# Preparing the first attention: query stacks in two buffers, rows normed one batch earlier, turned rows copied between the middle parts

## The reference, cut to what matters

```python
h = concatenate([token_mix(x), txt], axis=1)            # (8, 1056, 64), float32
h = h + attn(layernorm(h))                              # the first attention
def attn(x):
    qkv = (x @ qkv_w + qkv_b).reshape(B, N, 3, 8, 8)
    q, k, v = qkv[:, :, 0], qkv[:, :, 1], qkv[:, :, 2]
    attn = einsum('bnhd,bmhd->bhnm', q * 8 ** -0.5, k)
    bias = transpose(rpb_table[rel_idx], (2, 0, 1))      # by the distance of two rows
    attn = softmax(attn + bias[None], axis=-1)
    return einsum('bhnm,bmhd->bnhd', attn, v).reshape(B, N, 64) @ proj_w + proj_b
```

## Time and profile before

| what | value |
|---|---|
| median of 3 runs | 2847.63 us (2846.12 to 2851.1) |
| the profiled execution's own time | 2844.59 us |
| its span | 2842.8 us |
| mean granted TensorE clock | 0.899 of full speed |
| busy over the span | PE 88%, DVE 70%, ACT 53%, POOL 14% |
| store of qs, eight times, 1152 KB | 4.4 us to landing (median) |
| store of qT, eight times, 1056 KB | 4.4 us |
| store of kT, eight times, 1056 KB | 7.4 us |

### The profile page before, as it was taken

The page is one execution under the profiler, slowest core; times in us unless marked ns, Lnnn a source line. Parts: engine busy times, 40 slices in busy tenths (PEclk is TensorE's granted clock), DMA queues, the critical chain, the costliest instruction groups (busy, mean ns, idle before and its releaser), DMA issues. The chain is left out here.

```text
span 2842.8 us, 52541 instructions
## 1 busy us (share of the span) xinstructions
PE 2499.5 (88%) x18456; PEld 1092.8 (38%) x18456; DVE 1983.2 (70%) x5070; ACT 1519.3 (53%) x2629; POOL 400.8 (14%) x500
## 2 busy tenths in 40 slices
PE   5988657999999999997499999896679999599999
PEld 3323552333333333333333333564544444423333
DVE  5777667888888888883377776657676765266665
ACT  2331663777777777775144444334656667143443
POOL 1011210000000000002312111222100100411110
PEclk9998666999999999998599999665689999599999
DMA  2101751111111111122500100134441222701100
GB/s 75 23 15 24 239 203 58 48 48 32 48 46 34 48 41 39 48 45 48 111 12 19 25 15 21 48 94 125 154 139 61 81 62 57 155 12 30 30 21 15
DMA packets 272791, 174.02 MB, mean 61 GB/s; under 512 B 225857, under 2 KB 230786, under 8 KB 271282
## 3 DMA queue, kind: packets, MB, share of 16 engines
q1 hardware_dynamic: 262170, 151.59, 19.9%
q0 software_dynamic: 10368, 19.06, 2.2%
HBM read 96.11 MB, written 74.53 MB: 60 GB/s over the span
## 5 line engine op out<-in xcount | busy, mean ns | idle before, releaser
L1674 DVE TENSOR_REDUCE att_mpart<-ps 128x1 f32<-128x512 f32 x1024 | 635.6, 683 | 82.2 <-PE ps L1494 52.0
L1642 ACT ACTIVATE att_p<-ps 128x704 f32<-128x704 f32 x768 | 543.7, 760 | 136.1 <-PE ps L1558 131.8
L1587 PE MATMUL ps<-att_p,att_v 128*9 128x352 f32 x3072 | 300.5, 462 | 0.1
L1494 PE MATMUL ps<-att_kT,att_qT 64*128 64x512 bf16 x1024 | 276.4, 387 | 20.7 <-DMA att_qz<-qt_d 8.3
L1558 PE MATMUL ps<-att_qm,att_kT 64*128 64x352 bf16 x1536 | 251.9, 317 | 10.4 <-ACT att_p L1642 8.0
L1288 DVE TENSOR_REDUCE cau_mpart<-ps 128x1 f32<-128x512 f32 (+5 forms) x384 | 193.4, 552 | 80.3 <-PE ps L1114 60.9
L2419 ACT ACTIVATE mo_act<-ps,mo_b 128x768 f32<-128x768 f32 x176 | 156.3, 901 | 132.4 <-PE ps L2301 126.9
L2572 DVE TENSOR_TENSOR mo_g<-mo_act,ps 128x768 f32<-128x768 f32 x176 | 167.4, 951 | 77.8 <-PE ps L2336 41.2
L1255 ACT ACTIVATE cau_p<-ps 128x704 f32<-128x704 f32 (+6 forms) x272 | 171.5, 660 | 81.7 <-PE ps L1173 49.7
L2971 ACT ACTIVATE mo_act<-ps 128x1024 f32<-128x1024 f32 (+1 forms) x108 | 102.9, 953 | 195.0 <-PE ps L2885 194.8
L1558 PEld LDWEIGHTS ps<-att_qm,att_kT 64*128 64x128 bf16 x1536 | 82.8, 93 | 287.5 <-issue 278.0
(11 more groups left out here) (444 smaller groups left out, 4257.0 us busy)
## 6 DMA issues: line engine op xcount, KB each, us to landing
qs_d<-pre_qs SPq DMA_DIRECT2D x8, 1152.0 KB, 4.4
att_qs<-qs_d SPq DMA_DIRECT2D x32, 288.0 KB, 4.1
qt_d<-pre_qT SPq DMA_DIRECT2D x8, 1056.0 KB, 4.4
kt_d<-pre_kT SPq DMA_DIRECT2D x8, 1056.0 KB, 7.4
att_kT<-kt_d SPq DMA_DIRECT2D x32, 264.0 KB, 2.7
att_qT<-qt_d SPq DMA_DIRECT2D x32, 264.0 KB, 3.1
cqt_d<-cpr_qT SPq DMA_DIRECT2D x8, 1056.0 KB, 4.4
cau_qT<-cqt_d SPq DMA_DIRECT2D x16, 528.0 KB, 4.0
```

The costliest lines, as they stand in the source:

```text
L1494: mm = pe.matmul(ps[:, bank, :], qT[half(s), u, j * P:(j + 1) * P], kT[half(s), u, c * BANK:(c + 1) * BANK], start=True, stop=not near)
L1587: mm = pe.matmul(ps[32 * cg:32 * cg + DV, 7, 0:TH], v[:, u, i, s, :], p[:, r, s, :], start=i < 2, stop=i == FULL - 1)
L1642: e = act.activation(p[:, n % PRING, :, :], ps[:, bank:bank + 2, 0:TH], ACT.Exp)
L1674: red = dve.tensor_reduce(mpart[:, j, s, c:c + 1], ps[:, bank, :], AX.X, ALU.max)
```

## The change

The stacked queries get a second buffer. Rows are loaded three batches ahead, measured two batches ahead at the start of a step, and normed two batches ahead behind the fourth copy of turned queries. GpSimd takes the root of b + 2 after its middle parts, and sets up the second buffer behind root(1). ScalarE puts each of its three copies of turned rows in front of the middle parts 1, 2 and 3 of the keys, and waits for the `qs` store of two batches before in place of the last one. The loops are plain loops over b with the same steps.

```diff
@@ names @@
-        qs = nm.sb("qs", [P, NT, H * R], BF16)
+        qs2 = nm.sb("qs", [P, 2, NT, H * R], BF16)
+        qs = [qs2[:, i, :, :] for i in range(2)]
@@ SyncE @@
+            sp.wait_ge(xn_made, NT)
+            load(sp, 2, 0)
-            def step(b, par, more):
+            def step(b, par):
                 if b == 3:
                     ahead(sp, const)
-                if more:
-                    sp.wait_ge(xn_made, (b + 1) * NT)
-                    load(sp, b + 2, par)
+                if b + 3 < B:
+                    sp.wait_ge(xn_made, (b + 2) * NT)
+                    load(sp, b + 3, 1 - par)
@@ GpSimd @@
-            pool.memset(qs[:, :, :], 0.0).then_inc(zeroed, 1)
+            pool.memset(qs[0], 0.0).then_inc(zeroed, 1)
...
             pool.wait_ge(ones_set, 5)
+            root(1)
+            pool.memset(qs[1], 0.0).then_inc(spare_set, 1)
+            pool.wait_ge(spare_set, 1)
+            pool.memset(qh[1][:, :, :, 3:6], 1.0).then_inc(spare_set, 1)
+            pool.wait_ge(spare_set, 2)
             tidy(pool, const)
             for b in range(0, B):
-                if b + 1 < B:
-                    root(b + 1)
                 for m in range(NB):
...
-                    pool.tensor_copy(parts(qs, m, 3, 2), src.unsqueeze(2).broadcast_to([P, n * H, 2, D]))\
+                    pool.tensor_copy(parts(qs[b % 2], m, 3, 2), src.unsqueeze(2).broadcast_to([P, n * H, 2, D]))\
                         .then_inc(qmid_made, 1)
+                if b + 2 < B:
+                    root(b + 2)
@@ ScalarE @@
-            def copy_turned(b):
+            def copy_turned(b, chunks=range(3)):
                 at_least(act, qkv_mm, b * NB)
-                for c in range(3):
+                for c in chunks:
...
-                at_least(act, qs_out, b * 16)
+                at_least(act, qs_out, (b - 1) * 16)
+                if b == 1:
+                    act.wait_ge(spare_set, 2)
...
-                if not last:
-                    copy_turned(b + 1)
                 for m in range(NB):
                     n = tiles(m)
+                    if not last and 1 <= m < 4:
+                        copy_turned(b + 1, (m - 1,))
                     act.wait_ge(rest_made, b * 2 * NB + 2 * m + 2)
@@ VectorE @@
             def step(b, par, first, last):
-                if not last:
-                    measure(dve, b + 1, 1 - par)
-                    norm(dve, b + 1, 1 - par)
+                if b + 2 < B:
+                    measure(dve, b + 2, par)
...
                     dve.tensor_copy(qT[:, u, 0:TX], ps[:, (2 * u) % 3, :].bitcast(BF16)).then_inc(qt_cp, 1)
+                    if u == 3 and b + 2 < B:
+                        norm(dve, b + 2, par)
                 dve.wait_ge(qt_mm, b * 9 + 9)
...
-            by_two(dve, step)
+            measure(dve, 1, 1)
+            norm(dve, 1, 1)
+            for b in range(B):
+                step(b, b % 2, b == 0, b == B - 1)
```

More of the change, by code:

```diff
@@ L640, in heads_prep @@
          rstd_made, xn_made, xt_mm, xt_cp, qkv_mm, hi_made, rest_made, qmid_made, kmid_made, low_made, qt_mm, qt_cp, kt_cp,
-         tail_cp, vt_made, q_out, k_out, vt_out, qs_out) = nm.sems(
+         tail_cp, vt_made, q_out, k_out, vt_out, qs_out, spare_set) = nm.sems(
             "w_in", "w_scaled", "zeroed", "ones_set", "t_in", "t_split", "consts_set", "st_made", "agg_made",
@@ L644, in heads_prep @@
             "qmid_made", "kmid_made", "low_made", "qt_mm", "qt_cp", "kt_cp", "tail_cp", "vt_made", "q_out", "k_out", "vt_out",
-            "qs_out")
+            "qs_out", "spare_set")
         h_in_s = nm.sems("h_in0", "h_in1")
@@ L724, in step @@
                 sp.wait_ge(low_made, (b + 1) * 2 * NB)
-                sp.dma_start(qs_d[bass.ds(b, 1)].rearrange("b p n -> (b p) n"), qs[:, :, :].rearrange("p t n -> p (t n)"))\
+                sp.dma_start(qs_d[bass.ds(b, 1)].rearrange("b p n -> (b p) n"), qs[par].rearrange("p t n -> p (t n)"))\
                     .then_inc(qs_out, 16)
@@ L732, in step @@
                 sp.dma_start(kt_d[bass.ds(b, 1)].rearrange("b u p n -> p (b u) n"), kT[:, :, :]).then_inc(k_out, 16)
-            two_ahead(sp, step)
+            for b in range(B):
+                step(b, b % 2)
         @block.gpsimd
@@ L752, in _ @@
             pool.memset(v[:, :, :, :, :, D:D + 1].rearrange("p b u t s o -> p (b u t s) o"), 1.0).then_inc(ones_set, 1)
-            qh = qs[:, :, :].rearrange("p t (h r) -> p t h r", r=R)
+            qh = [x.rearrange("p t (h r) -> p t h r", r=R) for x in qs]
             kh = ks[:, :, :].rearrange("p t (h r) -> p t h r", r=R)
             pool.memset(kh[:, :, :, 0:3], 1.0).then_inc(ones_set, 1)
-            pool.memset(qh[:, :, :, 3:6], 1.0).then_inc(ones_set, 1)
+            pool.memset(qh[0][:, :, :, 3:6], 1.0).then_inc(ones_set, 1)
             pool.wait_ge(ones_set, 5)
+            root(1)
[3 more added lines that the diff above has]
+            pool.wait_ge(spare_set, 2)
             tidy(pool, const)
             for b in range(0, B):
-                if b + 1 < B:
-                    root(b + 1)
                 for m in range(NB):
@@ L809, in step @@
                     if c < 8:
-                        src, u = (ks if c % 2 else qs), c // 2
+                        src, u = (ks if c % 2 else qs[par]), c // 2
                         for t in range(FULL):
@@ L815, in step @@
                         apart(pe, const)
-                        for s, src in enumerate((qs, ks)):
+                        for s, src in enumerate((qs[par], ks)):
                             for u in range(4):
@@ L823, in _ @@
             turn(0)
-            by_two(pe, step)
+            for b in range(B):
+                step(b, b % 2, b == 0, b == B - 1)
         @block.scalar
@@ L845, in step @@
                     for j in range(n):
-                        for s, (x, slot0, step) in enumerate(((qs, 0, 1), (ks, 1, 2))):
+                        for s, (x, slot0, step) in enumerate(((qs[par], 0, 1), (ks, 1, 2))):
                             src = ps[:, 3 + m, j * 3 * C + s * C:j * 3 * C + (s + 1) * C].rearrange("p (h d) -> p h d", d=D)
@@ L875, in _ @@
             copy_turned(0)
-            by_two(act, step)
+            for b in range(B):
+                step(b, b % 2, b == 0, b == B - 1)
         @block.vector
@@ L904, in low @@
                 n = tiles(m)
-                for s, (x, got, slot, has) in enumerate(((qs, 5, 5, 3), (ks, 0, 0, 2))):
+                for s, (x, got, slot, has) in enumerate(((qs[b % 2], 5, 5, 3), (ks, 0, 0, 2))):
                     dve.wait_ge((qmid_made, kmid_made)[s], b * NB + m + 1)
@@ L919, in step @@
                         dve.wait_ge(vt_made, b + 1)
-                    for s, (x, has) in enumerate(((qs, 0), (ks, 1))):
+                    for s, (x, has) in enumerate(((qs[par], 0), (ks, 1))):
                         at_least(dve, low_made, (b - 1) * 2 * NB + 2 * m + s + 1)
```

## The result

The kernel after took 2841.41 us (median of 15 runs, 2837.36 to 2845.7); the kernel before took 2847.12 us in the 15 runs beside them. The ratio is 0.9978 with an interval of 0.997 to 0.9987: between 3.7 and 8.5 us faster. The forecast was 2839.5 us and a stage 8.1 us shorter. In the traces all of the gain comes from the stage of the change. The profiled execution took 2841.45 us (span 2839.7).

What follows compares the result with a forecast made beforehand. It took heads_prep, where no engine is full, to be bound by a ring of latencies. Seven steps summed to 120.1 us against 128.2 before, so 2847.63 - 8.1 = 2839.5 us; range 2833 to 2847.

Steps and rivals of the forecast that it cites:

- ring: heads_prep's chain of latencies, from batch 0's first query copy to batch 7's: 120.1 us forecast, 128.2 before.
- The memset holds the norm: Batch 0: second buffer's GpSimd memset delays VectorE's first norm; first stack transpose (T0) at 295.5 us, against 291.49 before.
- Rival 1: Batch 0: the memset holds nothing, so step 0 takes 15.75 us; kernel 2835.1 us; chance 0.20.
- The ring of steps 1 to 3: Batches 1 to 3, without the old waits: 15.55, 15.65 and 15.65 us; staying over 16.3 means the forecast fails.
- T to the next S: From a batch's first stack transpose on TensorE (T) to the next batch's first query copy (S): 7.1 us.
- rival 4: heads_prep: TensorE stays at its low clock, 1.65 us a step over six steps; kernel 2849.4 us; chance 0.10.
- 0.45 us less: Each batch, first query copy to first stack transpose: xT copies between middle key parts spread them, saving 0.45 us.
- Step 4: Batch 4: SyncE's queue delays batch 6's rows and batch 3's key store, which the key copies await; 18.8 us.
- Step 5: Batch 5: the corner's first part stands before measuring; some 10.4 us to first stack transpose, 17.7 in all.
- Steps 6 and 7: Batch 6, with a later corner part and no measuring: 16.55 us; batch 7 as before.
- Rival 2: Steps 1, 2, 3, 5 and 6: key store lands after 9.7 us and is awaited; kernel 2845.0 us; chance 0.12.
- Rival 3: Low parts held until GpSimd's root ends: 1.0 us in each of five steps; kernel about 2844.5 us; chance 0.08.

Runs made afterwards that it cites:

- The norm in the step: Kernel after with measuring, root, norm and loads back where they were before, only norm(1) ahead of the loop: 2850.81 us, 1.0011 of the kernel before.
- The 54 matmuls: Kernel after with float32-word memsets, ten pair loads in steps 5 and 6, and 54 unused bfloat16 identity matmuls a batch from batch 1: 2823.09 us, 0.9909 of before.
- words and late pairs: Kernel after with memsets written as float32 words and the next stage's ten pair loads issued in steps 5 and 6: 2834.15 us, 0.9947 of the kernel before.
- one stack: Kernel after without the second query buffer and its memset, ScalarE waiting for every stack store: 2843.51 us, 0.9980 of the kernel before.
- copies in front: Kernel after with the next batch's three xT copies back ahead of all middle key parts: 2840.33 us, 0.9981 of the kernel before.
- Moving the pair loads: Kernel after with the next stage's ten pair loads issued in steps 5 and 6 instead of step 3: 2836.36 us, 0.9966 of the kernel before.

## Why the prediction was right, and where it was not

**Moving the norm makes the gain: right.** The norm in the step, with the rest of the change in place, gave 129.6 us of ring against 121.4. But the earlier trace rows was read too widely. Its 14.3 us are no handover in every step: 7.7 stand at the stage's start and stayed, and the rest was in steps 5 and 6, where the gain is. Steps 1 and 2 fell by 0.3 and 0.2 us only (16.86 and 16.84 before).

**The memset holds the norm: right in kind, too long by 1.3 us.** T0 was S + 12.1, not 13.4. The prediction let T0 come 4.0 us later in the batch than before, for both memsets. The norms took 3.3 us more (5.41 - 2.10), the second memset held nothing, and S to T grew by 2.7 (9.44 to 12.13), so 0.6 of it was hidden. Rival 1 (nothing held) falls with the 4009 ns.

**The ring of steps 1 to 3: the failed step.** 15.55, 15.65 and 15.65 were given, and 16.53, 16.62 and 16.64 measured: 2.9 us of the sum. The prediction says that it fails if these batches stay over 16.3, and they do. Two terms of it were off, and no row gives the 0.1 less of step 1.
- "T to the next S is 7.1": it was 7.7 to 7.8, 2.0 us over three steps. I took it from batch 4 of before, where TensorE had idled 5.6 us and the clock still rose in the fifth group. The rise came in the sixth to eighth group of these three. This is the mechanism of rival 4, at 0.7 us a step of its 1.65: the clock does come up, only later. The 54 matmuls settle the clock as the cause: S to T and ScalarE's busy time stay the same (8.81; 12.18 us), and T to S falls to 5.8. What sets the group in a single batch stays open. The turn now stands directly behind the QKV, so TensorE idles in one piece of 5.7 us, but that is not shown to be the reason, and its length alone is not: in the kernel with words and late pairs batch 4 rose in the fourth group and batch 3 in the seventh, both after 5.68 us of idling; with one stack a batch that had idled 12.38 us rose in the fourth (T to the next S 6.76), and with the norm in the step one that had idled 3.44 rose in the seventh (7.79). The first transposes of those two batches:

```profile
360.22 1.01 PE L817 MATMUL ps<-eye,pre_qs 128*128 128x128 bf16 x8 [12.38 <-DVE pre_ks L914]
```

```profile
384.01 1.01 PE L818 MATMUL ps<-eye,pre_qs 128*128 128x128 bf16 x8 [3.44 <-DVE pre_ks L917]
```

- "0.45 us less" for copies between the parts: 0.15 to 0.2. S to T was 8.82; with the copies in front it was 8.97. (The prediction's own terms, 8.15, 0.3 and 0.15, make 8.6 and not 8.55.)

The Trainium skill (TensorE: Matmul & The Clock Gate, Part 4) has it that the full clock does not engage for transposes; batch 4 after, eight groups of 1.01 to 1.06 us, looks like it, but in every other batch transposes go from 1.06 to 0.61 among themselves, and in the last kernel they run at 0.61 from the first. The measurement decides: they can run at 2.4 GHz.

**Step 4: right for the reasons given.** 18.8 forecast, 19.33 measured. SyncE took 18.24 us between the two key stores (18.06 said), the rows came late (1.9 us of wait), the store of batch 3 landed after 9.9 us (9.7 said), and the first key copy waited 4.4. T was 1.1 sooner than said and the rest 1.7 longer. Of that, 1.5 came behind the landing (6.25 us to the next S, 4.8 said), with the last four transpose groups all at the low clock, 0.4 us more each. Moving the pair loads took the excess away.

**Step 5: 1.15 us less than said.** T came at S + 9.57, not 10.4. The key copies of batch 4 had waited, so norm and tails ended at S + 0.5 and not at S + 1.4, and the corner's piece started then.

**Steps 6 and 7: right.** 16.51 against 16.55, and step 7 as before (15.16 against 15.18).

**The other rivals.** Rival 2 (the key store as a wait in every step) falls: one wait of 4.4 us, in batch 4; the landing's median was 7.1. It is the next wait in line all the same: at 14.6 us a step it was back in two batches. Rival 3 (low parts held by the root) falls; the durations of the key low parts in steps 1 to 3 (ns min/median/max) and the root of step 1:

```profile
L920 DVE TENSOR_TENSOR pre_ks<-pre_rest,pre_ks x15: 217/292/379, 304.9 to 340.5; 128x128 bf16<-128x128 f32 x12, 128x64 bf16<-128x64 f32 x3
```

```profile
305.09 1.83 POOL L751 TENSOR_TENSOR pre_rstd<-pre_var,pre_half 128x9 f32<-128x9 f32 x1
```

The root ran from 305.09 to 306.92 with six low parts beside it, and none took over 0.38 us.

So the sum was short by 1.4 us: +2.9 in steps 1 to 3 and +0.5 in step 4, -0.8 in step 0 and -1.15 in step 5. That errors of 3.4 and 2.0 us had opposite signs is luck. The gain measured is 6.2 us by the ratio (3.7 to 8.5) and 5.7 by the medians, for a ring 6.7 us shorter.

## What to carry to other kernels

When a stage is a ring of latencies, look at when TensorE's clock comes back in each batch, and do not take its price from one: T to the next S went from 6.7 to 7.8 us between batches with the same 5.7 us of idling. Small bfloat16 matmuls on data that is at hand, released by the steps TensorE waits for anyway, held the clock at 1.00 over four steps and cost nothing where they ended before the awaited operand; where they did not, T came up to 0.8 us later. Count their time, since float32 ones of the same shape took more than the gain back. And place a wait of the view of waits in its step before calling it a cost of every step.

A buffer more is worth nothing where the wait it removes and the next one end at the same queue; look at what that queue issues between, and move what nobody needs yet. And price a memset by its elements and by the one VectorE instruction that it holds, not by all that stand beside it.

## What the runs showed of the hardware that was not expected

- GpSimd's memset went by elements: 128x4608 bfloat16 in 3.94 us, the same bytes as 128x2304 float32 in 2.02.
- One memset held one VectorE tensor-scalar instruction to its own end (4.01 us for a norm of 0.31; 2.05 for an add of 0.17) and was over then. The norm was held though it takes its scalars from SBUF. BATCH_NORM_STATS2 and BATCH_NORM_AGGREGATE beside the memset were not held, nor two-tensor low parts beside the root.
- Behind the same 5.7 us of idling TensorE's clock came up anywhere from the fourth to the eighth of eight transpose groups, behind 12.38 us in the fourth, and behind 3.44 us in the fifth to the seventh.
- 27 float32 matmul calls of 128x128 (54 records) took 6.29 us at the full clock; 28 bfloat16 ones within a longer stretch took 1.96.
